# A graph attention kernel: all source logits of the first layer looked up by TensorE instead of two fifths of them

## The reference

```python
xp = (x @ W).reshape(N, H, C)                      # N 3125, H 4, C 256
a_src = jnp.einsum('nhc,hc->nh', xp, att_src)
a_dst = jnp.einsum('nhc,hc->nh', xp, att_dst)
e = leaky_relu(a_src[src] + a_dst[dst], 0.2)       # per edge and head
m = segment_max(e, dst); ee = exp(e - m[dst]); z = segment_sum(ee, dst)
out = segment_sum(xp[src] * (ee / z[dst])[:, :, None], dst)
x = layernorm(x + relu(out + bias))
```

## Time and profile before

| | us |
|---|---|
| median of 3 runs | 2171.18 |
| lowest, highest | 2164.91, 2173.71 |
| profiled execution, span | 2761.9 |
| of it, stage one | 91 to 733 |

### The profile page before, as it was taken

The page is one execution under the profiler, slowest core; times in us unless marked ns, Lnnn a source line. Parts: engine busy times, 40 slices in busy tenths (PEclk is TensorE's granted clock), DMA queues, the critical chain, the costliest instruction groups (busy, mean ns, idle before and its releaser), DMA issues. The chain is left out here.

```text
span 2761.9 us, 52467 instructions
## 1 busy us (share of the span) xinstructions
PE 1865.4 (68%) x11779; PEld 1216.8 (44%) x11780; DVE 1524.7 (55%) x4081; ACT 862.2 (31%) x2923; POOL 1346.7 (49%) x1446
## 2 busy tenths in 40 slices
PE   5612119999857777777774886367677676856678
PEld 4300004444434555545553775244445444545544
DVE  5301006777655555555555996254544544678878
ACT  3000000000246666656564674100000000046656
POOL 1576770000046666666663112826666666147781
PEclk9855558999979999999998998688888888979999
DMA  8201002332168888888887994556766666478857
GB/s 302 49 2 21 4 15 72 98 91 87 44 203 297 295 291 291 291 292 295 291 293 239 306 308 145 145 154 193 192 194 190 194 194 195 141 218 310 308 187 267
DMA packets 256917, 531.76 MB, mean 193 GB/s; under 512 B 50253, under 2 KB 148694, under 8 KB 256782
## 3 DMA queue, kind: packets, MB, share of 16 engines
q0 software_dynamic: 95376, 276.01, 32.0%
q1 hardware_dynamic: 124142, 220.58, 23.8%
q10 hardware_dynamic: 37296, 33.96, 5.0%
HBM read 441.14 MB, written 102.23 MB: 197 GB/s over the span
## 5 line engine op out<-in xcount | busy, mean ns | idle before, releaser
L165 POOL DMA_INDIRECT acc<-xl_table,csrc x392 | 401.3, 1024 | 243.7 <-issue 110.7
L1274 ACT ACTIVATE wone<-onehot,w 128x64 f32<-128x64 f32 x1760 | 433.3, 333 | 278.3 <-DVE onehot L1320 174.0
L1291 PE MATMUL banks<-w_sb,wone 128*64 128x256 f32 x2368 | 346.6, 416 | 135.1 <-DVE acc L1316 42.1
L990 PE MATMUL banks<-w_sb,acc 128*128 128x512 f32 x736 | 367.1, 637 | 36.7 <-issue 36.5
L1768 PE MATMUL banks<-xr_parts,onehot_t 128*128 x1320 | 228.3, 314 | 241.3 <-issue 186.4
L165 POOL DMA_INDIRECT w_sb<-xp_table,isrc x296 | 294.5, 995 | 171.8 <-PE banks L1294 91.5
L1808 DVE SCALAR_TENSOR_TENSOR prod<-banks,att_relu 128x1024 f32<-128x1024 f32 x110 | 134.6, 1223 | 323.2 <-ACT w L1727 238.2
L1316 DVE TENSOR_TENSOR acc<-banks,acc 128x512 f32 x440 | 304.4, 692 | 0.0
L1768 PEld LDWEIGHTS banks<-xr_parts,onehot_t 128*128 128x128 bf16 x1320 | 137.3, 104 | 343.7 <-issue 302.3
L165 POOL DMA_INDIRECT ga<-a_src_table,csrc x240 | 239.4, 998 | 94.9 <-issue 76.6
L1291 PEld LDWEIGHTS banks<-w_sb,wone 128*64 128x64 f32 x2368 | 183.1, 145 | 193.5 <-issue 83.2
(11 more groups left out here) (336 smaller groups left out, 2966.0 us busy)
## 6 DMA issues: line engine op xcount, KB each, us to landing
edge_rows<-acc SPq DMA_DIRECT2D x440, 130.0 KB
rows<-edge_rows SPq DMA_DIRECT2D x55, 1040.0 KB, 5.0
lt_bc<-local_dst ACTq DMA_DIRECT2D x110, 128.0 KB
lt<-local_dst ACTq DMA_DIRECT2D x110, 128.0 KB
w<-acc SPq DMA_DIRECT2D x100, 128.0 KB, 3.4
x_table<-y POOLq DMA_DIRECT2D x25, 512.0 KB, 6.2
acc<-x_table SPq DMA_DIRECT2D x25, 512.0 KB, 3.7
acc<-in_x SPq DMA_DIRECT2D x12, 1024.0 KB, 14.7
```

Source lines behind the costliest of these rows:

```text
L165: return self.pool.indirect_dma_start(out, None, table, bass.IndirectOffsetOnAxis(ap=idx, axis=0), bounds_check=self.bound, oob_is_err=False)
L990: last = nc.tensor.matmul(psum[:, 2 * r + i], xT_all[:, u, k, :], w_sb[:, k, i * 512:(i + 1) * 512], start=(k == 0), stop=(k == KD - 1))
L1274: last = nc.scalar.activation(wone[:, s, j, h, :], onehot[:, s, j, :], ACT.Copy, scale=w9[:, bass.ds(g * U + j, 1), h:h + 1].rearrange("p ...
L1291: nc.tensor.matmul(psum[WN * a:WN * (a + 1), j, k * C:(k + 1) * C], wone[:, s, j, h, :], slots[r][:, j, h * C:(h + 1) * C], start=True, st ...
```

## The change

POOL's gathers of a_src, the table in HBM, its stores and its semaphores go. All 98 groups are looked up by PE. The source lookups take two PSUM banks in turn (6 and 7), low_bc is buffered five deep as lt_bc is and counts on the same semaphores, and each turn of DVE now has compare and pick in it. The projection is cut into slices of 3, 3, 3, 3 and 4 halves.

```diff
@@ setup: POOL, SP and DVE
-                    pool.wait_ge(s_csrc, 1)
-                    pool.wait_ge(s_as, 32)
-                    fetch_sources(pool, range(EARLY))
...
-                        for i, tiles in enumerate((slice(0, HALF), slice(HALF, NT))):
-                            sp.wait_ge(s_all, i + 1)
-                            sp.dma_start(as_rows[:, tiles, :], a_all[:, tiles, 0:H]).then_inc(s_as, 16)
...
-                    for n, i in enumerate(PICKS):
-                        nc.vector.tensor_copy(chi[:, n::2, :], psum[:, 5, 0:PICK_UNITS * GU * U]
-                                              .rearrange("p (q j) -> p q j", j=GU * U)[:, :, i * U:(i + 1) * U])
+                    nc.vector.tensor_copy(chi[:].rearrange("p q j -> p (q j)"), psum[:, 5, 0:NGC * U])
@@ stage one: buffers, POOL, ACT's queue
-            low_bc = sb("low_bc", [P, 2, U, P], BF16)
+            low_bc = sb("low_bc", [P, GU, U, P], BF16)
...
-                    fetch_sources(pool, range(EARLY, len(FETCHED) + 2))
...
-                    def load_low(u, n):
-                        wait(act, s_hl, 2 * u + n - 1)
+                    def load_low(q, i):
+                        wait(act, s_hl, q - (GU - 1))
...
@@ PE
-                    def look_up_sources(u, n):
-                        pe.wait_ge(s_hl, 2 * u + n + 1)
-                        wait(pe, s_hm, 2 * u + n)
+                    def look_up_sources(q, s):
+                        pe.wait_ge(s_hl, q + 1)
+                        wait(pe, s_hm, q - 1)
                         for j in range(U):
                             for k in range(PARTS):
-                                last = nc.tensor.matmul(psum[:, 6, j * NT * H:(j + 1) * NT * H], onehot_low[:, n, j, :],
+                                last = nc.tensor.matmul(psum[:, 6 + s, j * NT * H:(j + 1) * NT * H], onehot_low[:, s, j, :],
...
-                    SLICES = ((0, 2), (2, 4), (4, 6), (6, 7), (7, 8))
+                    SLICES = ((0, 3), (3, 6), (6, 9), (9, 12), (12, 16))
...
-                            if i in (1, 3) and static < PICK_UNITS:
-                                look_up_sources(u, i // 2)
-                            products(u + 1, 1 - r, k0, k1)
+                            if GU * static + i < NGC:
+                                look_up_sources(GU * u + i, (GU * r + i) % 2)
+                            halves(u + 1, 1 - r, n0, n1)
@@ DVE
-                        dve.reg_alu(last_group, chunks.regs[U - 1], 2, ALU.logical_shift_right)
-                        dve.reg_alu(group_of, last_group, 0, ALU.max)
                         dve.wait_ge(s_at, g + 1)
-                        wait(dve, s_hd, picks)
-                        dve.wait_ge(s_fetched, dve.snap(group_of, min_val=0, max_val=NGC - 1) + 1)
+                        dve.wait_ge(s_hd, min(g + 1, NGC) if isinstance(g, int) else g + 1)
...
-                    def pick_sources(u, n):
-                        dve.wait_ge(s_hp, 2 * u + n + 1)
+                    def pick_sources(q, s):
+                        dve.wait_ge(s_hh, q + 1)
+                        wait(dve, s_hd, q)
+                        dve.wait_ge(s_hp, q + 1)
...
-                    def turn(u, r, i, static, first=False, last=False):
...
+                    def turn(u, r, i, static):
+                        g, first, last = GU * u + i, GU * static + i, static == NU
+                        s, s1 = (GU * r + i) % 2, (GU * r + i - 1) % 2
                         if not last:
-                            onehots(g, i, (GU * r + i) % 2, u)
...
+                            onehots(g, i, s, u)
+                        if first < NGC:
+                            compare_sources(g, i, s, u)
+                        if first >= 1 and not (last and i > 0):
+                            reduce(g - 1, (i - 1) % GU, s1)
+                        if 1 <= first <= NGC:
+                            pick_sources(g - 1, s1)
+                        if first >= 1 + LAG:
+                            logits(g - 1 - LAG, (i - 1 - LAG) % GU, (GU * r + i - 1 - LAG) % 2)
```

More of the change, by code:

```diff
@@ L370, in gnn_kernel @@
         s_xp = sem("p1_xp")
-        s_ga = [sem(f"p1_ga{i}") for i in range(2)]
-        s_fetched = sem("p1_fetched")
-        EARLY = 1
         FIRST_K = 4
[L376 to L387, removed]
         with ExitStack() as ph:
@@ L977, in look_up_sources, with halves @@
                                                         as0[:, :, k, :], start=(k == 0), stop=(k == PARTS - 1))
                         last.then_inc(s_hp, 1)
-                    def products(u, r, k0, k1):
[L981 to L994, removed]
+                    def halves(u, r, n0, n1):
+                        if n0 == 0:
+                            wait(pe, s_xe, u - 1)
+                        for n in range(n0, n1):
+                            k, i = divmod(n, 2)
+                            if isinstance(u, int) and u == NT - 1:
+                                last = nc.tensor.matmul(
+                                    psum[WN * i:WN * (i + 1), 2 * r], xT_all[:, u, k, 0:WN],
+                                    w_sb[:, k, i * 512:(i + 1) * 512], start=(k == 0), stop=(k == KD - 1))
+                                continue
+                            last = nc.tensor.matmul(
+                                psum[:, 2 * r + i], xT_all[:, u, k, :],
+                                w_sb[:, k, i * 512:(i + 1) * 512], start=(k == 0), stop=(k == KD - 1))
+                        if n1 == 2 * KD:
+                            last.then_inc(s_xp, 1)
@@ L996, in _ @@
+                    def products(u, r, k0, k1):
+                        halves(u, r, 2 * k0, 2 * k1)
                     for k in range(FIRST_K, KD):
@@ L1065, in _, with loaded @@
                     chunks = StepTiles(dve, ctab, "p1_c", U, NGC * U)
[L1066 to L1067 removed]
+                    def loaded(i, m):
+                        both = m + 1 if not isinstance(m, int) else min(m + 1, -(-(NGC - i) // GU))
+                        return 16 * (m + 1) + 16 * both
                     def onehots(g, i, s, m):
[L1070 removed]
+                        dve.wait_ge(s_lt[i], loaded(i, m))
                         wait(dve, s_pg, g - 1)
@@ L1124, in evict_xp @@
                                                 bias_bc[:], ALU.add).then_inc(s_xe, 1)
-                    def turn(u, r, i, static, first=False, last=False):
-                        g = GU * u + i
+                    def turn(u, r, i, static):
+                        g, first, last = GU * u + i, GU * static + i, static == NU
+                        s, s1 = (GU * r + i) % 2, (GU * r + i - 1) % 2
                         if not last:
-                            onehots(g, i, (GU * r + i) % 2, u)
-                        if not (first and g < 1) and not (last and i > 0):
-                            reduce(g - 1, (i - 1) % GU, (GU * r + i - 1) % 2)
-                        if not (first and g < 1 + LAG):
-                            k = i - 1 - LAG
-                            done = 2 * (u if k >= 0 else u - 1) + sum(k % GU >= i for i in PICKS)
-                            if static:
-                                done = min(done, NPICK)
-                            logits(g - 1 - LAG, k % GU, (GU * r + k) % 2, done)
+                            onehots(g, i, s, u)
[7 more added lines that the diff above has]
+                            logits(g - 1 - LAG, (i - 1 - LAG) % GU, (GU * r + i - 1 - LAG) % 2)
                     def unit(u, r, static):
@@ L1156, in _ @@
                         for r in range(2):
-                            unit(2 * pair + r, r, 0)
+                            unit(2 * pair + r, r, 2)
                     for u in range(2 * (PICK_UNITS // 2), NU):
@@ L1160, in _ @@
                     for i in range(LAG + 1):
-                        turn(NU, NU % 2, i, True, last=True)
+                        turn(NU, NU % 2, i, NU)
                         if i == 1:
```

61 lines of the change are left out of this document (22 added, 39 removed).

## The result

The changed kernel takes 2213.40 us (median of 4 runs, 2207.79 to 2214.49), the kernel before beside it 2169.89 us (4 runs): a ratio of 1.0197, with a 95% interval of 1.0181 to 1.0214. That is 43.5 us more, against 53 forecast.

A forecast was written before the change was run, and what follows sets the result against it. The prediction took PE to bound stage one in timed runs, with DVE becoming the bound. Lookups and picks 51 + 2 = 53 us, gathers, setup, loads and loop 0: 2171 + 53 = 2224 us, range 2160 to 2266.

The forecast's parts named there:

- DVE becomes the bound: Stage one: 60 more compares and picks bring DVE to 18.4 us a unit, above PE's 17.4; 53 us in all.
- PE's floor of 17.4 us: Stage one: 60 more groups looked up by PE raise its unit from 15.73 to 17.4 us, 33 us in all.
- Even slices 0: Projection in stage one: even slices move no matmul in or out of a unit, so 0 by themselves.
- More loads 0: ACT's queue in stage one: 98 instead of 38 low_bc loads, covered by being called four turns early, 0.
- The larger loop body 0: DVE's eight-fold loop in stage one: longer code might stall at jumps, 0 to 19 us; taken as 0.
- One bank would have chained them: Source lookups: a single PSUM bank would chain matmuls, picked, matmuls; the second bank covers PE's wait. No size given.
- At most 37 us of stall in the timed runs: Stage one: of the profile's 284 us stall at least 247 are missing from timed runs, leaving at most 37.
- 344 us at most: Later gather stages: the most they could give of the 590.7 us gap, 125 from weighted sum, 219 from second-layer logits.
- The span of 2531 us after the change: Profile of the changed kernel: 2761.9 us less the 284 us stall plus 53 us, about 2531 us.
- The rule on the gap between profile and time: Skill's rule that a profile's total stands about 6.2 us above execution time; judged not to hold, the gap being 590.7 us.
- Rival B: Stage one: the stall is in timed runs too, so removing gathers gives 1940 us, or 2082 for half; chance 0.13.
- The gathers are the stall: Stage one: the profile's stall of 284 us belongs to the a_src gathers and goes when they are removed.

The follow-up runs named there:

- experiment 3: Changed kernel with the high one-hot made for the first two groups only, taking work from DVE and none from PE: 2513.64 us, ratio 0.9104 to the kernel before.
- experiment 4: Changed kernel with the third bf16 part left out of the source lookups, taking work from PE and none from DVE: 2522.20 us, ratio 0.9143 to the kernel before.
- experiment 11: Changed kernel with the four esum adds moved from DVE to POOL: 2534.50 us, ratio 0.9099 to the kernel before on the same chip.
- experiment 12: Changed kernel with one group in five gathered by POOL, spaced behind PE's lookups, the other four looked up by PE: 2499.06 us, ratio 0.9041 to the kernel before.
- experiment 10: Kernel before with only the even slices of the projection put in: 2787.09 us beside 2786.72, ratio 1.0008.
- experiment 5: Changed kernel with one more small reduce in each turn of DVE: 2560.98 us, ratio 0.9257 to the kernel before, 36.7 us above the changed kernel.
- experiment 9: Changed kernel with one PSUM bank instead of two for the source lookups: 2524.48 us, ratio 0.9135 to the kernel before.
- experiment 1: Kernel before, unedited, timed and profiled again on a slower chip: 2761.88 us beside 2758.79 for the same kernel, ratio 1.0003.
- experiment 2: Changed kernel, unedited, on a slower chip: 2524.27 us beside 2763.38 for the kernel before, ratio 0.9125.
- experiment 6: Changed kernel with 240 gathers of a_src put back, back to back into a spare tile nobody waits for: 2831.66 us, ratio 1.0243 to the kernel before.
- experiment 7: Changed kernel with 120 back-to-back gathers into a spare tile nobody waits for: 2687.70 us, ratio 0.9648 to the kernel before.
- experiment 8: Changed kernel with 98 spare gathers, one a turn, each released by PE's lookup of a group: 2544.89 us beside 2786.72 for the kernel before, ratio 0.9136.

## Why the prediction was right or wrong

The forecast, slower with DVE as the new bound, held: +43.5 us for +53, inside the range of 2204 to 2266 us and the wider one from 2160. By its own steps:

- **DVE becomes the bound: right,** shown by experiments 3, 4 and 11. I had a unit of 18.4 us; it is 18.0 in the mean of 97 turns. The term was over-sized by 0.2 us a turn: I read a pick turn of 3.42 us out of the kernel before; in the new order a turn is 3.22. The reduce of dst with the adds and writes took 0.27 + 0.90 us there, and takes 0.17 + 0.80 now (307.19 to 307.36, 308.91 to 309.71). The wait of pick's reduce for the product, which I named, makes no difference: product and reduce are 1.55 us in both. Against the 0.2 stand about 0.4 us after each eviction (305.68) and 0.55 us at each jump back, which I had at nearly nothing and at nothing. In part the errors cancel, and that much of the near hit is luck.
- **PE's floor of 17.4 us: right** (17.34 in experiment 11, where nothing holds PE up; 16.80 for 16.83 in experiment 12). That the page would show PE at 94% was wrong: it shows 99.7%, as the waits fall inside groups. DVE over 90%: 292.23 of 321 is 91%.
- **Even slices 0: right** for the kernel before (experiment 10). **More loads 0: right** as far as the waits show: none on low_bc or lt_bc is among those of stage one.
- **The larger loop body 0: right for this kernel,** 4.1 us in eight jumps, and 2.7 us in six in the kernel before (from 425 us on). How close the edge was I did not know: ten instructions more cost 22 us (experiment 5), just outside the 19 us that I kept for it.
- **"One bank would have chained them": wrong.** One bank costs 0.2 us, nothing that can be told (experiment 9). PE waits 8.8 us in all for it, inside its slack to DVE.
- **At most 37 us of stall in the timed runs: the bound held, its reading was wrong.** I took the 590.7 us between profile and median as something that a profiled execution has and a timed one lacks. They were of two chips, as far as the record shows: a quick and a slower one. On a slower chip timed runs have the stall as well (experiment 1), on the quick one neither a profile of the changed kernel nor the timed runs show it: 284 - 282.6 = 1.4 us remain by the difference of the differences (experiment 2). The step that failed is the question "is it in the timed runs too?", which named only two answers. The argument of what the later stages can give at most did not depend on that, and it carried the forecast: 344 us at most, 311 measured. It was closer than it looks: the weighted sum alone gave 128 us where I had allowed 125.
- **The span of 2531 us after the change: wrong** for the profile that came (2209.9 us), since that was taken on the quick chip. On a slower chip, where that sum was made, the span is 2522.4 us.
- **The rule on the gap between profile and time.** Execution time less span is 2.8 us in the changed kernel's profile and 1.6 us in experiment 1. Beside this, the Trainium skill ("Runtime: NRT & Kernel Launch", the ~15µs preamble/postamble breakdown) gives a gap of about 6.2 us with the profile's total as the longer; here the span is the shorter one, so the sign and the size are not seen in these runs. That the two differ by a few microseconds, the same for every kernel, agrees with them. I was wrong to set it aside, and wrong to conclude that by it the stall would be the timed runs' own: a gap of 590.7 us between two numbers that should differ by a few says that they are not of the same conditions.
- **Rival B, the stall is the timed runs' own,** had 0.13. For the measured pair it is false. On the slower chips it is what happens: -239 us, where B's working gave -231.
- **The gathers are the stall: right,** and no wait for their data is needed for it: their unbroken train does it, on the slower chips (experiments 6 to 8).

Left open: why such a train stops the other engines, and why only on some chips. The waits are put down to "issue" and "remote", and the bytes are few; no run here opened it further. The kernel before was not profiled on a quick chip, so that it has no stall there rests on the sum in experiment 2. No experiment ran on the quick chip either; what experiments 3, 4, 9 and 11 say of the measured pair rests on stage one of the changed kernel being the same on both, 384.6 and 384.7 us.

## What to carry to other kernels

When a profile and the timed runs differ by more than a few microseconds, ask first whether both were taken on the same chip, and compare differences between kernels on one chip before explaining the gap by a mechanism. An engine that a view shows at 99.7% can still be the one that waits: take a little work from each suspect in turn, and see which the time follows. Where a helper's gathers can't be avoided, spread them behind the main engine's own steps instead of issuing them in a train.

## What the runs showed of the hardware

- On the slower chips a back-to-back train of small gathers (1.30 us apart) costs the kernel 1.21 to 1.28 us a gather, with PE busy 58 and DVE 19 of 321 us while it runs, though nobody waits for the data and the DMA share is 0.08; with some 3.3 to 3.7 us between starts the cost can't be measured. On the quick chip the sum in experiment 2 leaves 1.4 us for 240 of them.
- The same chips run the gathers of the weighted sum in 697 us where the quick chip takes 569, and the second layer's logits in 712 where it takes 532.
- A loop's jump back cost DVE 0.5 us, and 3.3 us a jump in the mean once ten instructions had been added to its body, with 33 more packets on instruction queue 14 in eight jumps.
